# The first head pair taken from a projection with repeated columns, and expert slots matched on VectorE and ScalarE

## The reference

```
xn   = layernorm(x)                                   # over the 128 features, no affine
q,k,v = xn@Wq+bq, xn@Wk+bk, xn@Wv+bv                  # 16 heads of 8 features
attn = softmax(q k^T / sqrt(8)) v                     # per batch and head, 1024 x 1024
a    = attn@Wo + bo
logits = xn @ router_w.T                              # 8 experts
top 2 experts of each token, g = sigmoid(top values) / their sum
f    = sum over the two of g_e * (silu(xn@w_gate[e]) * (xn@w_up[e])) @ w_down[e]     # 256 hidden
out  = x + a + f
```

## Time and profile before

| | |
|---|---|
| median of 3 runs | 870.05 us (868.89 to 873.38) |
| the profiled execution's own time | 869.59 us |
| its span | 867.9 us |
| PE busy | 819.4 us, 94% |
| DVE busy | 740.4 us, 85% |
| ACT busy | 694.4 us, 80% |
| POOL busy | 471.3 us, 54% |
| chain that ended last, by engine | PE 81%, DVE 13%, ACT 2%, issue 2%, DMA 2%, SP's queue 1% |

### The profile page before, as it was taken

One profiled execution on the slowest core, in us unless ns is written; L12 is line 12 of the kernel. 1 busy time (PEld: TensorE's weight loads), 2 busy tenths in 40 slices (PEclk: granted clock), 3 DMA queues, 4 the chain that ended last, 5 costly groups with the idle time before them and its releaser, 6 DMA issues.

```text
span 867.9 us, 20181 instructions
## 1 busy us (share of the span) xinstructions
PE 819.4 (94%) x6725; PEld 446.6 (51%) x6725; DVE 740.4 (85%) x1380; ACT 694.4 (80%) x1521; POOL 471.3 (54%) x670
## 2 busy tenths in 40 slices
PE   8996767789999999999999999999999999999997
PEld 7762222335555555555555555555555555555533
DVE  6579998999888978989989888988888888898834
ACT  3453645579898988989989898888998988898885
POOL 3442008024576756767667656766666756666410
PEclk9996877999999999999999999999999999999999
DMA  4678077022343333333443433333334343332133
GB/s 119 173 238 263 5 151 49 15 65 69 91 92 90 82 80 80 72 98 75 100 93 89 100 82 87 86 77 91 84 75 99 80 99 95 87 96 61 39 91 111
DMA packets 94952, 80.92 MB, mean 93 GB/s; under 512 B 19560, under 2 KB 84320, under 8 KB 94816
## 3 DMA queue, kind: packets, MB, share of 16 engines
q1 hardware_dynamic: 80336, 67.51, 29.9%
q0 software_dynamic: 13632, 11.79, 9.1%
q10 hardware_dynamic: 880, 0.33, 0.3%
HBM read 57.99 MB, written 22.71 MB: 93 GB/s over the span
## 4 chain that ended last, share of the span: by engine, by line
PE 81%; DVE 13%; ACT 2%; issue 2%; DMA 2%; SPq 1%; ACTq 0%; DVEq 0%
PE ps L1176 27%; PE ps L1161 17%; PE ps L1151 15%; PE ps L1223 7%; DVE maxima L957 6%; PE ps L1206 6%; PE ps L1189 2%; ACT probs L667 1%; PE ps L1063 1%; DVE xnT L943 1%; PE ps L1212 1%; PE ps L1239 1%; PE ps L1183 1%; DMA gu_w<-L_ffn_w_up 1%; DVE stage L934 1%
## 5 line engine op out<-in xcount | busy, mean ns | idle before, releaser
L957 DVE TENSOR_REDUCE maxima<-ps 128x1 f32<-128x512 f32 x1024 | 638.5, 684 | 74.7 <-PE ps L1161 69.8
L667 ACT ACTIVATE probs<-ps 128x512 f32<-128x512 f32 x1024 | 537.9, 610 | 107.5 <-PE ps L1151 103.9
L1161 PE MATMUL ps<-qk 64*128 64x512 f32 x1024 | 392.5, 441 | 36.2 <-DVE maxima L957 34.0
L1151 PE MATMUL ps<-qk 64*128 64x512 f32 x1024 | 381.9, 462 | 2.2 <-ACT probs L667 1.9
L1161 PEld LDWEIGHTS ps<-qk 64*128 64x128 f32 x1024 | 183.8, 188 | 175.0 <-DVE maxima L957 142.9
L1176 PE MATMUL ps<-probs,v_all 128*9 128x512 f32 x2048 | 271.8, 603 | 1.7 <-ACT o_sb L673 1.1
L1151 PEld LDWEIGHTS ps<-qk 64*128 64x128 f32 x1024 | 179.8, 188 | 23.8 <-ACT probs L667 14.9
L565 POOL DMA_INDIRECT acc<-result,idx x71 | 117.6, 1656 | 114.5 <-issue 93.9
L1223 PE MATMUL ps<-xg_T,gu_w 64*128 64x128 f32 x1136 | 155.4, 276 | 0.1
L1223 PEld LDWEIGHTS ps<-xg_T,gu_w 64*128 64x128 f32 x1136 | 145.6, 187 | 9.2 <-ACT result L694 9.0
L1206 PEld LDWEIGHTS ps<-dn_w,hid 64*128 64x128 f32 x568 | 74.4, 186 | 62.4 <-ACT probs L667 51.5
(11 more groups left out here) (152 smaller groups left out, 608.9 us busy)
## 6 DMA issues: line engine op xcount, KB each, us to landing
gu_w<-L_ffn_w_gate SPq DMA_DIRECT2D x71, 128.0 KB
gu_w<-L_ffn_w_up SPq DMA_DIRECT2D x71, 128.0 KB
dn_w<-L_ffn_w_down SPq DMA_DIRECT2D x71, 128.0 KB
qk<-q_parts SPq DMA_DIRECT2D x124, 64.0 KB
qk<-k_parts SPq DMA_DIRECT2D x124, 64.0 KB
k_parts<-stage SPq DMA_DIRECT2D x24, 256.0 KB, 3.5
q_parts<-stage SPq DMA_DIRECT2D x16, 256.0 KB, 3.5
x_sb<-L_attn_inputs SPq DMA_DIRECT2D x4, 512.0 KB, 8.9
```

The costliest lines, as they stand in the source:

```text
L667: act.activation(probs[:, u % NPB, q, h, :], ps[:, BANK_OF[job], :], ACT.Exp).then_inc(s_read, 1)
L957: dve.tensor_reduce(maxima[:, p % 2, qt, h, k:k + 1], ps[:, x_bank(i), :], AX.X, ALU.max, negate=True).then_inc(x_read, 1)
L1151: pe.matmul(ps[:, bank, :], t[r, 1, kt * P:(kt + 1) * P], t[r, 0, q * CH:(q + 1) * CH], start=True, stop=True).then_inc(s_filled, 1)
L1161: pe.matmul(ps[:, bank, :], t[r, 0, qt * P:(qt + 1) * P], t[r, 1, k * CH:(k + 1) * CH], start=True, stop=True).then_inc(x_filled, 1)
```

## The change

Two things are changed together.

1. *The first pair.* The weight columns of heads 0 and 1 of Wq and Wk are copied four times into `w_rows` (ACT, `spread_weights`), so that a projection gives q or k of both heads already repeated in the rows where `qk[0]` wants them. Four such projections (q and k of chunks 0 and 1, `FIRST_ROWS`) stand ahead of the units. ACT writes each twice: whole, and multiplied by a 0/1 column that is 1 on the rows for lo. DVE masks the upper bits of the first and adds or subtracts (a column of +1 and -1) with the second, straight into `qk[0]`; the rows of padding come from the zero weights and a bias of 0 or 1. Four small DMAs bring the repeated biases; they wait for a memset of DVE and stand on ACT's queue ahead of `rw_in`, `bo_row` and `wo`. `copy_part` goes, and so do BRIDGE and FILL. The ordinary jobs of chunks 0 and 1 move into the units: q0, k0, q1, k1, lg0, lg1 in slots 0 to 5, v0 and v1 in slots 18 and 19; those of chunks 2 to 7 move back by 2 or 3 slots, the last (k7, v7) into unit 0. DVE's statistics and moments of the rest move into unit -12, the reciprocal into unit -11, ACT's root and norm behind k1.
2. *Matching.* POOL's four instructions over 2304 elements become 32 over 288; `lower` becomes four instructions over 128 columns for each one over 512, and covers chunks 0 and 1 as well. `match_places` on DVE covers the first choice only (4 calls, units 12, 14, 16, 18). The second choice is matched on ACT, units 11 to 18 (`places`): |r - place| for 4 tiles, one instruction each, then relu(1 - that) for the four together. DVE computes one more small row (`minus_place`) in unit 8.

```diff
 # SP
-            sp.wait_ge(hi_ready, 2)
-            for h in range(2):
-                copy_part(sp, 0, h, 0)
 ...
-            store_parts(0)
-            store_parts(1)
-            for p in range(1, NQ - 1):
-                load_pair(p)
             for u in UNITS:
                 if u - 1 in UPPER_AT:
                     store_parts(UPPER_AT[u - 1])
+                    if UPPER_AT[u - 1] == 1:
+                        for p in range(1, NQ - 1):
+                            load_pair(p)
 # POOL
+            for c in range(NC):          # lower(c): four pieces of 128 columns for each of q and k
                 lower(c)
+                if c in (1, 3, 5):
+                    pool.wait_ge(lo_ready, 2 * c + 2)
+                    pads((c + 1) // 2)
+            def number_tiles(i):
+                k, n = i // 8, slice(4 * (i % 8), 4 * (i % 8) + 4)
 ...
+            pool.wait_ge(match_step, 4)
+            for i in range(16):
+                number_tiles(i)
 # ACT
+            act.wait_ge(sign_step, 2)
+            for z, b in enumerate((bq, bk)):
+                for h in range(2):
+                    act.dma_start(row_bias[64 * h:64 * h + 32, 0, z:z + 1],
+                                  b[D * h:D * h + D].rearrange("(a d e) -> a d e", a=1, e=1).broadcast_to([4, D, 1])).then_inc(rows_bias, 16)
             act.dma_start(rw_in[:, :], router_w).then_inc(small_in, 16)
             act.dma_start(bo_row[:, :], ...)
             act.dma_start(wo[:, :], Wo).then_inc(wo_in, 16)
 ...
+            def take_rows_of_first(job, c):
+                z = ("rows_q", "rows_k").index(job)
+                act.wait_ge(s_filled, s_full(job, c))
+                act.activation(probs[:, c, z, 0, :], ps[:, BANK_OF[job, c], :], ACT.Identity, bias=row_bias[:, 0, z:z + 1],
+                               scale=(SCALE, 1.0)[z])
+                act.activation(probs[:, c, z, 1, :], ps[:, BANK_OF[job, c], :], ACT.Identity, bias=row_bias[:, 1, z:z + 1],
+                               scale=row_scale[:, z:z + 1]).then_inc(s_read, 1)
 ...
+            def places(i):
+                n0 = 4 * i
+                if i == 0:
+                    act.wait_ge(slots_known, 1)
+                for n in range(n0, n0 + 4):
+                    ins = act.activation(at_places[:, 1, n, :], iota_b[:, :], ACT.Abs, bias=minus_place[:, n:n + 1])
+                ins.then_inc(far_ready, 1)
+                act.wait_ge(far_ready, i + 1)
+                act.activation(at_places[:, 1, n0:n0 + 4, :], at_places[:, 1, n0:n0 + 4, :], ACT.Relu, scale=-1.0,
+                               bias=ones_f[:, 0:1]).then_inc(places_too, 1)
 # DVE
             norm(0)
 ...
+            dve.wait_ge(rows_bias, 16 * 4)
+            dve.tensor_scalar(row_bias[:, 0, 0:1], row_bias[:, 0, 0:1], SCALE, None, ALU.mult).then_inc(const_step, 1)
 ...
             norm(1)
 ...
             statistics(1)
             statistics(2)
 ...
+            def rows_of_first(n, job, c):
+                z = ("rows_q", "rows_k").index(job)
+                dve.wait_ge(s_read, s_taken(job, c))
+                all_of, lo_of = probs[:, c, z, 0, :], probs[:, c, z, 1, :]
+                dve.tensor_scalar(all_of.bitcast(I32), all_of.bitcast(I32), TOP, None, ALU.bitwise_and).then_inc(sign_step, 1)
+                dve.wait_ge(sign_step, 8 + n + 1)
+                dve.scalar_tensor_tensor(qk[0][:, z, c * CH:(c + 1) * CH], all_of, row_sign[:, z:z + 1], lo_of,
+                                         ALU.mult, ALU.add).then_inc(pair_ready, 1)
 ...
                 if u in UPPER_AT:
                     upper(UPPER_AT[u])
+                    if UPPER_AT[u] == 0:
+                        rest_moments()
+                    if UPPER_AT[u] == 1:
+                        rest_rstd()
 # PE, ahead of the units: turn 0, turn 1, GAP, bias product, then
+            pe.wait_ge(rows_w, 3)
+            for job, c in FIRST_ROWS:
+                z = ("rows_q", "rows_k").index(job)
+                project(job, c, w_rows[:, z].rearrange("p h n d -> p (h n d)"))
 ...
+                if p == 0:
+                    pe.wait_ge(pair_ready, 4 if qt >= TPC else 3 if k == 1 else 2)
 # the table of slots
+SLOTS = [("q", 0), ("k", 0), ("q", 1), ("k", 1), ("lg", 0), ("lg", 1)]
+SLOT_OF = {job: n for n, job in enumerate(SLOTS)} | {("v", 0): 18, ("v", 1): 19}
+    SLOT_OF |= {("turn", _c): 2 * _c + 2, ("lg", _c): 2 * _c + 3, ("q", _c): 3 * _c + 2, ("k", _c): 3 * _c + 3, ("v", _c): 3 * _c + 4}
-    for _job, _slot in (("turn", 2 * _c - 1), ("lg", 2 * _c), ("q", 3 * _c - 1), ("k", 3 * _c), ("v", 3 * _c + 1)):
+MATCH_AT = {9: (0, 1), 10: (2, 3)} | {12 + 2 * i: (4 + i,) for i in range(4)}
+PLACES_AT = {11 + i: i for i in range(8)}
```

More of the change, by code:

```diff
@@ L43 @@
 GAP = 4
-BRIDGE = 22
-FILL = 4
 TOP = -4096
@@ L222, in build @@
         tile_e = early[:, 8 * NT * NE:8 * NT * NE + TILES * NE].rearrange("p (t e) -> p t e", e=NE)
+        minus_place = early[:, 3 * NT * NE:3 * NT * NE + NT]
         zeros = early[:, 2688:2688 + RW]
@@ L325, in loads_done @@
         def loads_done(p):
[L326 to L333, removed]
+            return LOADS * (p // NQ + (1 if p % NQ else 0))
         block = ctx.enter_context(nc.Block())
@@ L500, in _ @@
-            for c in REST:
-                lower(c)
[L503 to L506, removed]
+                    for n in range(4):
+                        r = slice(n * CH // 4, (n + 1) * CH // 4)
+                        ins = pool.tensor_tensor(lo_st[:, s, z, r], qk_st[:, s, z, r], hi_st[:, s, z, r], ALU.subtract)
@@ new lines, in lower @@
+                    ins.then_inc(lo_ready, 1)
+            for c in range(NC):
+                lower(c)
+                if c in (1, 3, 5):
[3 more added lines that the diff above has]
+                k, n = i // 8, slice(4 * (i % 8), 4 * (i % 8) + 4)
+                one, nth = in_tiles[:, k, n, 1, :], in_tiles[:, k, n, 0, :]
+                pool.tensor_tensor(nth, one, iota_b[:, n.start + 1:n.stop + 1].rearrange("p (n a) -> p n a", a=1).broadcast_to([P, 4, TILES]),
@@ L513, in _ @@
-            for k in range(2):
-                number_tiles(k)
+                pool.wait_ge(tiles_ready, 2 * i + 2)
+            pool.wait_ge(match_step, 4)
+            for i in range(16):
+                number_tiles(i)
             def clear_shift(p):
@@ L634, in take_chunk_job, with spread_weights @@
                     take_k(c)
+                    if c == 1:
+                        root(1)
+                        norm(2)
                 if job == "v":
                     take_v(c)
+            def spread_weights(z):
+                w = (wq, wk)[z]
+                act.activation(w_rows[:, z, :, 0:4, :], w[:, 0:2 * D].rearrange("p (h a d) -> p h a d", h=2, a=1).broadcast_to([P, 2, 4, D]),
+                               ACT.Copy).then_inc(rows_w, 1)
+            def take_rows_of_first(job, c):
[5 more added lines that the diff above has]
+                               scale=row_scale[:, z:z + 1]).then_inc(s_read, 1)
             root(0)
+            act.wait_ge(proj_in, 48)
+            act.wait_ge(rows_w, 1)
+            for z in range(2):
+                spread_weights(z)
             act.wait_ge(rw_T, 1)
@@ L840, in _, with rest_moments, rest_rstd @@
             dve.tensor_tensor(bo_row[:, :], bo_row[:, :], ps[:, 5, 0:E], ALU.add).then_inc(bo_ready, 1)
+            def rows_of_first(n, job, c):
[6 more added lines that the diff above has]
+                                         ALU.mult, ALU.add).then_inc(pair_ready, 1)
+            for n, job in enumerate(FIRST_ROWS):
+                rows_of_first(n, *job)
+            rest = slice(NT // B, NT)
+            def rest_moments():
+                statistics(3)
+                dve.wait_ge(stat_done, NT)
+                moments(rest)
+            def rest_rstd():
+                dve.wait_ge(std_ready, 2)
+                dve.reciprocal(mom[:, 1, rest], mom[:, 4, rest]).then_inc(rstd_ready, 1)
+                dve.wait_ge(rstd_ready, 1)
+                dve.scalar_tensor_tensor(mom[:, 5, rest], mom[:, 0, rest], -1.0, mom[:, 1, rest], ALU.mult, ALU.mult).then_inc(rstd_ready, 1)
             rank_bc = rank[:, :].rearrange("p (a e) -> p a e", a=1).broadcast_to([P, NT, NE])
@@ L918, in route @@
                     then(dve.tensor_copy(tile_of[:, :, :], slot_i[:, 1]))
+                    then(dve.scalar_tensor_tensor(minus_place, tile_of[:, 1, :], float(P), slot_f[:, 1, :], ALU.mult, ALU.subtract))
                     dve.scalar_tensor_tensor(place_of[:, :, :], tile_of[:, :, :], -float(P), slot_f[:, :, :], ALU.mult, ALU.add).then_inc(slots_known, 1)
@@ L1126, in slot_rows @@
                 bank = s_room("idx") if i == 0 else BANK_OF["idx",]
-                pe.wait_ge(places_ready, i + 1)
-                pe.wait_ge(tiles_ready, 4)
+                if i < 4:
+                    pe.wait_ge(places_ready, i + 1)
+                else:
+                    pe.wait_ge(places_too, 2 * (i - 4) + 2)
```

(1 more changed line is left out.)

131 lines of the change are left out of this document (49 added, 82 removed).

## The result

| | before | after |
|---|---|---|
| median (4 runs each) | 869.94 us (868.89 to 873.38) | 881.08 us (880.23 to 882.75) |
| span of the profiled execution | 867.9 us | 878.6 us |
| unit -12 starts | 29.90 | 21.58 |
| unit -9 | 39.90 | 37.01 |
| unit -3 | 63.58 | 68.31 |

The account below looks back on a forecast made before the run. PE was taken as full from unit 24, so the gain is how much earlier that starts: 3.6 us at unit 11 plus 0.3 is 3.9; 869.6 less 3.9 is 865.7, plus 0.46 for the median 866.2 us, range 860.5 to 872.

Parts of the forecast that it names:

- first maximum: Start of unit -12: DVE's first maximum at 23.4 for 29.9, 6.5 us gained (5.3 to 8.5).
- units -12 to -10: Longer DVE list, PE idle some 4 us, lower clock in unit -10: 3.1 left of the 6.5 us.
- units -9 to -4: Set by PE: two turns and a logits group more, one k and one v less, +0.1 us; 3.0 left.
- units -3 to 0: `lower` in pieces gives 2.0 us back, k7 in unit 0 costs 1.2: +0.8, 3.8 left.
- units 1 to 10: The row `minus_place` costs 0.2 us; 3.6 left at unit 11.
- units 11 to 23: Stall of unit 11 goes, ACT sets the pace at 4.1 us a unit: 51.0 for 51.3, +0.3 us.
- covered by 1.6 us only: POOL's 32 pieces end at 147.6; PE wants them at the end of unit 16, 149.2 at the earliest.
- The sign of being wrong: ACT having gaps in units 11 to 18 would show the forecast wrong, with a larger gain.
- The stall that doesn't go: POOL's pieces grow to 0.8 us and more, PE waits 2.3 in unit 16, `lower` gains nothing: 870.5; chance 0.05.
- ACT's rival: Units 11 to 18: ACT's matches cost 2.74 us a call, a unit 4.8, eight lose 5.9: 872.1; chance 0.13.
- 44.8 us for all matches on DVE: Units 11 to 23 with matches left on DVE and only POOL's pieces made small, before any wait for POOL.

Follow-up runs that it names:

- e4: The change with POOL's numbering in 16 instructions over 576 elements in place of 32 over 288: 876.44 us, 1.0087.
- e2: The kernel before with only the second part of the change (matching on ACT, small POOL pieces, `lower` in quarters): 870.49 us, 1.0019.
- e7: The kernel before with the second part of the change, but POOL's numbering in 16 instructions over 576 elements: 865.28 us, 0.9959.
- e8: The kernel before with only POOL's numbering in 16 instructions over 576 elements; matches stay on DVE, `lower` whole: 868.71 us, 1.0007.
- e14: The kernel before with the second part, 16 POOL pieces, PE waiting for its own pieces, and 46 more filler products in units -3 to 0: 868.77 us, 0.9991.
- e10: The kernel before with the second part, POOL's numbering in 16 pieces, and PE waiting for its own pieces only: 865.23 us, 0.9959.
- e12: The kernel before with its filler products on PE taken out (1 for each 22 and 1 for 4), nothing else: 872.97 us, 1.0037.
- e11: The change with padding in one go behind lower(1), 16 POOL pieces, PE waiting for its own, and filler in slots 1 to 4, 6, 7: 868.76 us, 0.9996.
- e5: The change with POOL's padding of pairs 1 to 3 written in one go behind lower(1): 876.91 us, 1.0108.
- e9: The change with PE's product of slot rows waiting only for POOL's pieces of its own token tiles, not all 32: 876.08 us, 1.0085.

## Why the prediction was wrong

It said 866.2, with no change above 0.5% (0.51) or a gain (0.42) as the likely outcomes; it is 881.1, outside the range (860.5 to 872), and no rival was near. Its steps, with what the trace after has in their place (gains positive, in us):

| step | predicted | measured |
|---|---|---|
| first maximum | +6.5 | +8.3 |
| units -12 to -10 | -3.4 | -5.4 (15.4 for 10.0) |
| units -9 to -4 | -0.1 | -7.6 (31.3 for 23.7) |
| units -3 to 0 | +0.8 | -2.2 (23.5 for 21.3) |
| units 1 to 10 | -0.2 | -1.3 |
| units 11 to 23 | +0.3 | -2.9 (54.3 for 51.3) |
| sum | +3.9 | -11.2 |

**First maximum: right, and the surplus was luck.** `bo_row`'s wait ended at 11.99 (said: near 12), a call of ACT took 0.69 to 0.81. The surplus of 1.8 us lies ahead of the projections, which start at 14.19 (said: 16.0), and it comes from PE's clock. Before, then after:
```profile
12.00:14.00 2.00, 2.00 (x10) 1.65 (x9) 2.00 (x12) 0.60 (x1) 0.28 (x2) 0.53 0.31 84
12.00:14.00 2.00, 2.00 (x18) 1.98 (x19) 2.00 (x12) 1.26 (x3) 0.77 (x3) 1.00 0.01 4
```
The edit doesn't explain that. e4 has the same start as the change, its clock was 0.58 there and its first maximum came at 23.24. Profiles with the old start show the same two cases: 27.5 to 27.9 at full clock (e2, e7, e8, e14), 29.5 to 30.0 with the lower clock (before, e10, e12). Like compared with like, the new start gains 5.7 to 6.8 us, where the forecast had 6.5.

**Units -12 to -10: right in kind, too small.** I priced the lower clock in one unit only. It stayed at 0.50 for 20 us, into unit -8. e12 shows that taking filler away costs 3.8 us in these units by itself; e11 shows that giving it back keeps the clock. The moments too took 0.36 to 0.43 beside POOL's pieces, 0.18 to 0.20 otherwise.

**Units -9 to -4: the step that failed.** "Their slots 6 to 17 now hold [a little more] and one k and one v less: +0.1" counted PE's jobs at full clock and nothing else. Two things were missing. The clock, which made units -9 and -8 11.1 us long for 8.5. And the padding: the diff moves `pads` of pairs 2 and 3 from the first maxima to behind lower(3) and lower(5), and I never asked what stands beside it there. It stood beside DVE's masks; unit -5 took 6.6 us for 4.0, and unit -4, with PE run dry for 0.9 us and the clock at 0.62, 5.2 for 2.8. e5 moves the padding, the masks take 0.75 again, and this stretch takes 28.4 us in its profile, 2.9 less; units -9 and -8, where the clock is at 0.50 as in the change, stay at 11.1. My rule, "a DVE instruction with two inputs waits for the end of POOL's", was too narrow, since the mask has one input and POOL's memset reads nothing. The Trainium skill ("SBUF — State Buffer", Who interferes with whom) says that VectorE's tensor_scalar, in a mode that uses both ports, takes the port pair that GpSimd uses, and that a tensor_reduce never does on this chip. The times in the trace agree, 2.29 us for 0.75 and 0.62 for 0.62; in which mode the masks ran, no run shows.

**Units -3 to 0.** The gain by `lower` in quarters is real: 2.3 us in e7, where I took 2.0. In the change it is buried. One cause is the second block of memsets (1.99 for 0.75 at 76.77). The larger piece is unit 0, to which k7 and v7 moved: it takes 7.1 us for 4.9, and 7.2 in e5, where the masks are short. The clock is 0.50 from 76 to 84 us in both kernels, but in the change PE is busy for all of the 8.00 us in place of 5.17. That unit 0 is longer because of k7 and v7 at that clock is read from the profiles, not tested by a run. Units 1 to 10 lost 1.3 us; that was not followed up.

**Units 11 to 23.** The stall of unit 11 went, and ACT's price was right (Abs 1.28 for four and relu 0.72, at 3.85 us a unit with the exponentials; said 2.04 and 4.1). What failed was the margin: "covered by 1.6 us only". POOL's 32 pieces took 26.5 us and not 23.0 (three of them 1.53 to 1.65 beside DVE's matches, and 0.75 from one to the next), and PE came for them 19.6 us after the start of unit 11 (156.06), not 24.6, because the units before 16 ran at 3.5 us and not at ACT's full pace. Together a wait of 7.2. e4 and e9, which take it away in two different ways, give 4.6 and 5.0 us by the medians. The sign of being wrong came up too: ACT has a gap in unit 16 (4.95 us, for PE), though not with the larger gain that was written beside it.

**The rivals.** The stall that doesn't go had the right mechanism, POOL's pieces late in unit 16, but 2.3 us for 7.2 and a chance of 0.05. The side on which the case lay, a slower kernel, had 0.07. ACT's rival had a slip in its sum: eight units at 4.8 for 4.1 us are 5.6 more, not 5.9. The prediction's 44.8 us for all matches on DVE left out waits for POOL. e8 measured 50.6, and PE waits 2.54 us for POOL in its unit 16; e7, with half of the matches on ACT, took 50.8. The Trainium skill ("ScalarE: Activation LUTs", Rules for kernel authors) says to use VectorE, not ScalarE, for relu and the like; in this stretch it made no difference. No run has all matches on DVE and PE waiting for its own pieces only.

**Added up.** By the medians padding 4.2, pieces 4.6 and filler 3.4 bring the change from 881.1 to 868.8. The second part alone, mended, is 865.2. So the first part still costs 3 to 3.5 us, although the first maximum comes 4 to 7 us earlier in those profiles than in the ones without the first part (23.2 to 23.3 against 27.5 to 30.0). The profiles of e11 and e10, both with the lower clock at 12 to 16 us, say where it goes: the first maximum is 6.3 us earlier, units -12 to -10 are 4.7 longer, -9 to -4 2.8, -3 to 0 3.4, and units 1 to 23 1.1 shorter; that makes 3.5 at unit 24. In the first of these lie q, k and the logits of chunks 0 and 1, which PE did before the first maximum while the copies were under way. In the second the padding is not mended after all. Written in one go it now stands beside the masks of unit -8 (DVE, then POOL, of e11):
```profile
45.54 2.45 DVE L839 TENSOR_SCALAR stage<-stage 128x512 int32<-128x512 int32 x2
...
36.57 12.30 POOL L462 MEMSET qk<- 32x1024 f32 x12
```
That is 1.7 of the 2.8 us. In the third unit 0 takes 7.4 us for 4.9, as above. So the jobs moved behind the first maximum are not shown to be the whole of what is left, and no run has all of the padding out of the masks' way together with the filler.

## What to carry to other kernels

Work taken off the way to the first result has to go somewhere: price the stretch that takes it in, with the clock that it will have there, before counting the gain. When a block of one engine moves, look at what runs beside it in its new place; in this kernel VectorE and GpSimd stretched each other, also where one only filled memory. Before a gain at the start is put down to an edit, compare profiles that had the same clock there. And where a consumer waits for many small pieces, let it wait for its own, and check the margin with the consumer at its earliest.

## What the runs showed of the hardware that was not expected

- PE can be recorded as busy for a whole stretch and stay at the lower clock: 8.00 of 8.00 us from 36 to 44, clock 0.50 (change); the same stretch is at 1.00 with filler ahead of it and in it (e11).
- The clock at the start differs between profiles of kernels that have the same start: 1.00 or 0.58 in 12 to 14 us (change, e4), and with it the first maximum at 21.58 or 23.24.
- GpSimd's memset over 32x1024 (about 1.0 us) stretches VectorE's masks over 128x512: 2.29 and 1.99 us for two in place of 0.75. VectorE's match over 128x1024 stretches GpSimd's piece in turn: 0.67 to 1.53, 1.15 to 2.21.
- GpSimd's cost for the numbering is 0.67 us over 288 elements and 1.15 over 576, with 0.07 to 0.08 between two: small pieces cost 0.19 us each beyond their elements (2 x 0.67 - 1.15).
- A full clock isn't worth its price everywhere: e14 kept it at 1.00 to 84 us, where DVE was busy 19.26 of the 20.00 us from 64 to 84 without that filler (e10), and lost about 3 us.
